# Moving a router's part boundaries, one batch's gather to GpSimd's queue and its transpose to TensorE

## The reference, cut to what matters

```python
x = L0_attn_x                                  # (8, 512, 128): 8 batches of 512 tokens
x = x + attn(layernorm(x))                     # 16 heads, causal softmax, then sa @ Wp + bp
h = layernorm(x)
shared = (silu(h @ shared_gate.T) * (h @ shared_up.T)) @ shared_down.T
probs = sigmoid(h @ router_w.T + routing_bias) # 8 experts, the top 2 of each token
w = the two probs over their sum, 0 for the other six experts
combined = sum over e of w[:, e] * ((silu(h @ gate_w[e]) * (h @ up_w[e])) @ down_w[e])
return x + shared + combined
```

## Time and profile before

| what | value |
|---|---|
| median of 3 runs | 767.33 us (763.23 to 767.85) |
| the profiled execution | 765.89 us |
| its span, first to last instruction | 764.1 us |
| PE, DVE, ACT, Pool busy | 659.3, 538.8, 459.9, 304.5 us |
| matmuls | 5426 |

### The profile page before, as it was taken

The page is one execution under the profiler, slowest core; times in us unless marked ns, Lnnn a source line. Parts: engine busy times, 40 slices in busy tenths (PEclk is TensorE's granted clock), DMA queues, the critical chain, the costliest instruction groups (busy, mean ns, idle before and its releaser), DMA issues. The chain is left out here.

```text
span 764.1 us, 16403 instructions
## 1 busy us (share of the span) xinstructions
PE 659.3 (86%) x5426; PEld 398.2 (52%) x5426; DVE 538.8 (71%) x1900; ACT 459.9 (60%) x817; POOL 304.5 (40%) x508
## 2 busy tenths in 40 slices
PE   7478999999989998999999998996788789888920
PEld 6354455545545554454555554553377677577610
DVE  6799777787788788878778778762057755667914
ACT  3366667757757766667867766673475546556600
POOL 3493512314223223463322322367600067666671
PEclk9799999999999999999999999999899899999955
DMA  9102335411110311230210210134155543764322
GB/s 249 46 2 64 90 108 149 144 57 57 46 56 29 74 36 36 75 114 26 80 51 29 59 32 28 40 78 103 36 120 113 113 108 111 142 120 123 101 67 83
DMA packets 104849, 61.07 MB, mean 80 GB/s; under 512 B 45960, under 2 KB 96544, under 8 KB 104768
## 3 DMA queue, kind: packets, MB, share of 16 engines
q1 hardware_dynamic: 68336, 29.34, 15.9%
q10 hardware_dynamic: 32336, 22.29, 9.5%
q0 software_dynamic: 4096, 8.40, 4.3%
HBM read 19.88 MB, written 31.06 MB: 67 GB/s over the span
## 5 line engine op out<-in xcount | busy, mean ns | idle before, releaser
L1256 ACT ACTIVATE p_sb<-bank,inv_scale 128x512 f32<-128x512 f32 (+1 forms) x384 | 221.9, 614 | 34.3 <-PE bank L1018 27.1
L1370 DVE CUSTOM_DVE_ANT_0 junk<-bank,causal 128x512 bf16<-128x512 f32 (+3 forms) x512 | 221.2, 483 | 23.6 <-PE bank L995 23.3
L904 POOL TENSOR_SCALAR_AFFINE_SELECT p_sb<-p_sb 128x384 f32<-128x384 f32 x128 | 66.9, 522 | 303.5 <-ACT p_sb L1256 303.3
L1017 PE MATMUL bank<-ql,ah 128*128 128x512 f16 (+3 forms) x512 | 153.7, 300 | 0.0
L1018 PE MATMUL bank<-qh,al 128*128 128x512 f16 (+3 forms) x512 | 153.2, 300 | 0.0
L995 PE MATMUL bank<-ah,qh 128*128 128x512 f16 (+3 forms) x512 | 132.1, 302 | 23.6 <-DVE low L1370 22.2
L1016 PE MATMUL bank<-qh,ah 128*128 128x512 f16 (+3 forms) x512 | 147.5, 301 | 1.2 <-ACT p_sb L1256 1.2
L1342 DVE TENSOR_TENSOR ql<-bank,qh 128x512 f16<-128x512 f32 x128 | 88.5, 691 | 68.9 <-ACT qh L1221 65.2
L1221 ACT ACTIVATE qh<-bank 128x512 f16<-128x512 f32 x128 | 76.4, 597 | 63.3 <-PE bank L960 61.7
L1546 DVE SCALAR_TENSOR_TENSOR al<-bank,gu_scale,ah 128x512 f32<-128x512 f32 x69 | 51.6, 748 | 72.9 <-ACT ah L1287 56.6
L995 PEld LDWEIGHTS bank<-ah,qh 128*128 128x128 f16 x512 | 50.0, 98 | 82.2 <-DVE low L1370 49.7
(11 more groups left out here) (234 smaller groups left out, 1162.0 us busy)
## 6 DMA issues: line engine op xcount, KB each, us to landing
o_dram<-oT ACTq DMA_DIRECT2D x32, 256.0 KB, 2.3
ys_dram<-ql ACTq DMA_DIRECT2D x25, 256.0 KB
xs_dram<-causal ACTq DMA_DIRECT2D x6, 832.0 KB, 4.6
wst<-in_Wkqv SPq DMA_DIRECT2D x8, 264.0 KB, 5.3
x_sb<-in_x SPq DMA_DIRECT2D x8, 256.0 KB, 6.0
o_all<-o_dram SPq DMA_DIRECT2D x8, 256.0 KB
r_all<-r_dram SPq DMA_DIRECT2D x8, 256.0 KB
x_dram<-rows SPq DMA_DIRECT2D x8, 256.0 KB, 2.3
```

Of the source, the lines that this page charges most:

```text
L904: nc.gpsimd.affine_select(out=three, in_=three, compare_op=ALU.is_ge, fill=0.0, base=0, pattern=[[0, 3], [1, P]], channel_multiplier=-1).t ...
L1017: nc.tensor.matmul(bank, m.ah[:, keys], ql[:, s, c * P:N], start=False, stop=False)
L1256: nc.scalar.activation(p_sb[v % P_RING][:, S_AT[k]:S_AT[k] + S_WIDTH[k]], m.psum[S_BANK[k]][:, 0:S_WIDTH[k]], ACT.Exp, scale=m.inv_scale[: ...
L1370: last = nc.vector.tensor_tensor_reduce(out=junk[:, (3 * u + k) % 2, at:at + w], in0=m.psum[M_BANK[(3 * u + k) % 2]][:, at:at + w], in1=m. ...
```

## The change

It does five things. The parts become 3, 2 and 3 batches. The steps behind a batch's attention are put into other slots, most of them earlier and several into one; the sort's pieces get slots of their own. For batch 7 the gather of sums and products and the spread of the inverses are issued by Pool's own queue, in slot 144, and SP no longer has them. Batch 7's normed rows are transposed by PE (`late`, slot 150) and copied from the bank by ACT and DVE (`late_copy`, slot 151) in place of the store and the two transposing loads. The logits of batch 6 stand in slot 141 and their exponentials are taken in slot 152, together with batch 7's; the buffer `lg` gets two halves for that.

The slots that come of it (batch b < 6: from slot 29 + 16 b):

| step | before | after |
|---|---|---|
| rinv, mult, proj, stats of batch b | +2, +4, +6, +6 | +0, +2, +4, +6 |
| aggr, newton, norm, split, logits of b | +8, +10, +11, +14, +18 | +6, +6 and +7, +8, +10, +14 |
| sort of the first part | 67, 71 | 79 (three pieces), 80, 81, 82, 83 |
| its sends | 76 to 83 (16) | 88 to 99 (24) |
| sort of the second part | 115, 119 | 111 (three pieces), 112, 113, 114, 115 |
| its sends | 124 to 135 (24) | 120 to 127 (16) |
| batch 6: mult, proj, norm, split, logits | 129, 131, 136, 139, 143 | 127, 129, 133, 135, 141 |
| batch 7: rinv, mult, proj | 142, 145, 147 | 144, 144, 148 |
| batch 7: norm, logits; third sort, place, first send | 148, 154; 155, 158, 159 | 149, 152; 153, 156, 157 |

```diff
@@ -32,7 +32,7 @@
 HN_RING = 6
 W_BOUND = 4096.0
 GU_BOUND = 32.0 / W_BOUND ** 2
-SPLITS = ((0, 8), (8, 20), (20, 32))
+SPLITS = ((0, 12), (12, 20), (20, 32))
 PARTS = len(SPLITS)
 CHUNK = P // E
 CHUNKS = tuple(tuple((t, min(t + CHUNK, t1)) for t in range(t0, t1, CHUNK)) for t0, t1 in SPLITS)
@@ -448,14 +448,18 @@
 
 SORTS = 7
 PLACE_LATE = -(-(PV_AT - LOW_AT) // GROUP)
-STEPS = {"rinv": 2, "mult": 4, "proj": 6, "stats": 6, "aggr": 8, "newton0": 10, "newton1": 10, "newton2": 10, "norm": 11, "split": 14, "logits": 18}
-LAST_STEPS = {"rinv": 1, "mult": 4, "proj": 6, "stats": 6, "aggr": 6, "newton0": 7, "newton1": 7, "newton2": 7, "norm": 7, "split": 8, "logits": 13}
-PART_STEPS = {"sort": 22, "weigh": 26, "count": 27, "rank": 30, "place": 30, "expert": 34, "send": 31}
-LAST_PART_STEPS = {"sort": 14, "count": 16, "weigh": 16, "rank": 17, "place": 17, "expert": 18, "send": 18}
+STEPS = {"rinv": 0, "mult": 2, "proj": 4, "stats": 6, "aggr": 6, "newton0": 6, "newton1": 7, "newton2": 7, "norm": 8, "split": 10, "logits": 14}
+LATE_LOGITS = 16
+LAST_STEPS = {"rinv": 3, "mult": 3, "proj": 7, "stats": 7, "aggr": 7, "newton0": 8, "newton1": 8, "newton2": 8, "norm": 8, "late": 9, "late_copy": 10, "logits": 11, "split": 12}
+PART_STEPS = {"sort": 18, "weigh": 22, "count": 23, "rank": 26, "place": 26, "expert": 30, "send": 27}
+LAST_PART_STEPS = {"sort": 12, "weigh": 13, "count": 14, "rank": 15, "place": 15, "expert": 16, "send": 16}
+SORT_LATE = ((0, 0, 0, 1, 2, 3, 4), (0, 0, 0, 0, 1, 1, 1))
 
 
 def step_at(name, b):
 
+    if (name, b) == ("logits", B - 2):
+        return step_at("rinv", b) - STEPS["rinv"] + LATE_LOGITS
     return PV_AT + H - GROUP + 2 + H * b + (STEPS if b < B - 1 else LAST_STEPS)[name]
 
 
@@ -467,12 +471,17 @@
 
 def sort_at(k, g):
 
-    return part_step_at("sort", g) + k // 4 * (GROUP if g < PARTS - 1 else 1)
+    return part_step_at("sort", g) + SORT_LATE[g == PARTS - 1][k]
 
 
 def batch_at(name, t):
 
     return next((b for b in range(B) if step_at(name, b) == t), None)
+
+
+def late_at(name, t):
+
+    return step_at(name, B - 1) == t
 
 
 def part_at(name, t):
@@ -805,9 +813,11 @@
                 inverses = m.r_dram[b * P:(b + 1) * P, :].rearrange("(h c) n -> h (c n)", h=H)
                 sp.dma_start(r_all[:, :], inverses.unsqueeze(1).to_broadcast([H, DH, N])).then_inc(r_placed, 16)
 
-            def turn_rows(b):
+            def store_rows(b):
                 sp.wait_ge(xl_ready, b + 1)
                 sp.dma_start(m.x_dram[b * N:(b + 1) * N, :].rearrange("(t p) d -> p t d", p=P), rows[:, b % HN_RING, :, :]).then_inc(x_stored, 16)
+
+            def turn_rows(b):
                 sp.wait_ge(x_stored, 16 * (b + 1))
                 if b >= 1:
                     sp.wait_ge(x_turned, 16 * 2 * b)
@@ -853,12 +864,8 @@
                     for b in range(t0 // TB, t1 // TB):
                         sp.wait_ge(rows_sent[b], 16 * 2 * TB)
                 if q == X_RING:
+                    store_rows(B - 2)
                     turn_rows(B - 2)
-                    gather_products(B - 1)
-                if q == X_RING + 1:
-                    spread_inverses(B - 1)
-                if q == LAST_TURN:
-                    turn_rows(B - 1)
                 if q >= X_RING:
                     sp.wait_ge(gate_up, quad_ends[q - X_RING])
                 for k, x in enumerate((xsh, xsl)):
@@ -905,9 +912,25 @@
                     one = p[:, P_AT[1]:P_AT[1] + P]
                     nc.gpsimd.affine_select(out=one, in_=one, compare_op=ALU.is_ge, fill=0.0, base=0, pattern=[[1, P]], channel_multiplier=-1).then_inc(p_masked, 1)
 
+                if late_at("rinv", t):
+                    for k in range(2):
+                        pool.wait_ge(o_stored[k], 16 * H // GROUP // 2 * B)
+                    pool.wait_ge(rinv_ready, B - 1)
+                    pool.wait_ge(on_ready, B - 1)
+                    heads = m.o_dram[(B - 1) * H // GROUP * P:B * H // GROUP * P, :].rearrange("(h c) n -> h c n", h=H)
+                    pool.dma_start(sums[:, :], heads[:, DH, :]).then_inc(late_sums_placed, 16)
+                    pool.dma_start(o_all[:, :], heads[:, 0:DH, :]).then_inc(late_o_placed, 16)
+                    pool.wait_ge(rinv_ready, B)
+                    pool.dma_start(m.r_dram[(B - 1) * P:B * P, :], rinv[:, :]).then_inc(late_r_stored, 16)
+                    pool.wait_ge(late_r_stored, 16)
+                    inverses = m.r_dram[(B - 1) * P:B * P, :].rearrange("(h c) n -> h (c n)", h=H)
+                    pool.dma_start(r_all[:, :], inverses.unsqueeze(1).to_broadcast([H, DH, N])).then_inc(late_r_placed, 16)
+                if late_at("mult", t):
+                    pool.wait_ge(late_r_placed, 16)
+                    pool.wait_ge(late_o_placed, 16)
                 if (b := batch_at("mult", t)) is not None:
-                    pool.wait_ge(r_placed, 16 * (b + 1))
-                    pool.wait_ge(o_placed, 16 * (b + 1))
+                    pool.wait_ge(r_placed, 16 * min(b + 1, B - 1))
+                    pool.wait_ge(o_placed, 16 * min(b + 1, B - 1))
                     if b >= 1:
                         pool.wait_ge(t_filled, T_TURN["proj", b - 1] + 1)
                     nc.gpsimd.tensor_tensor(onT[:, :], o_all[:, :], r_all[:, :], ALU.mult).then_inc(on_ready, 1)
@@ -1048,11 +1071,18 @@
                     for i in range(TB):
                         last = nc.tensor.matmul(bank_t[:, i * P:(i + 1) * P], onT[:, i * P:(i + 1) * P], m.wp[:, :], start=True, stop=True)
                     last.then_inc(t_filled, 1)
+                if late_at("late", t):
+                    turn("late", 0)
+                    pe.wait_ge(hn_ready, B)
+                    for i in range(TB):
+                        last = nc.tensor.transpose(bank_t[:, i * P:(i + 1) * P], hn[:, i, :], m.ident[:, :])
+                    last.then_inc(t_filled, 1)
                 if (b := batch_at("logits", t)) is not None:
                     turn("logits", b)
                     if b == 0:
                         pe.wait_ge(scale_chain, SCALE_LINKS)
-                    pe.wait_ge(x_turned, 16 * 2 * (b + 1))
+                    if b < B - 1:
+                        pe.wait_ge(x_turned, 16 * 2 * (b + 1))
                     for i in range(TB):
                         at = slice((b * TB + i) * P, (b * TB + i + 1) * P)
                         logits = bank_t[:, i * E:(i + 1) * E]
@@ -1111,8 +1141,10 @@
                 if u >= DEEP:
                     pe.wait_ge(gu_ready, u - DEEP + 1)
                 if unit.shared:
-                    if unit.half == 0:
+                    if unit.half == 0 and unit.batch < B - 1:
                         pe.wait_ge(x_turned, 16 * 2 * (unit.batch + 1))
+                    elif unit.half == 0:
+                        pe.wait_ge(t_taken, T_TURN["late", 0] + 1)
                     for kind, bank in ((0, GB), (1, UB)):
                         at = E * EW + kind * I + unit.half * P
                         last = three(m.psum[bank[u % DEEP]], 0, wh[:, at:at + P], wl[:, at:at + P], xh[:, seg(unit.batch, N)], xl[:, seg(unit.batch, N)])
@@ -1294,11 +1326,16 @@
                     quad, q = unit.quad, unit.quad.q
                     act.wait_ge(yst_ready, q + 1)
                     act.dma_start(m.ys_dram[quad.part][quad.rows, :].rearrange("(j p) d -> p j d", p=P), yst[:, q % X_RING, 0:quad.n * D].rearrange("p (j d) -> p j d", d=D)).then_inc(ys_stored[q % X_RING], 16)
+                if late_at("late_copy", t):
+                    act.wait_ge(t_filled, T_TURN["late", 0] + 1)
+                    act.wait_ge(wl_ready, KINDS * (E + 1))
+                    nc.scalar.activation(xh[:, seg(B - 1, N)], bank_t[:, :], ACT.Copy, scale=LIFT).then_inc(late_xh_ready, 1)
                 if t >= FFN_AT:
                     split_rows(t)
-                if (b := batch_at("logits", t)) is not None:
-                    act.wait_ge(t_taken, T_TURN["logits", b] + 1)
-                    nc.scalar.activation(ex[:, seg(b, TB), :], lg[:, :, :], ACT.Exp, scale=-1.0).then_inc(ex_ready, 1)
+                for b in range(B):
+                    if step_at("logits", max(b, B - 1) if b == B - 2 else b) == t:
+                        act.wait_ge(t_taken, T_TURN["logits", b] + 1)
+                        nc.scalar.activation(ex[:, seg(b, TB), :], lg[:, b % 2, :, :], ACT.Exp, scale=-1.0).then_inc(ex_ready, 1)
 
         @block.vector
         def _(dve):
@@ -1329,6 +1366,11 @@
                     dve.wait_ge(t_filled, T_TURN["rank", g] + 1)
                     n = len(CHUNKS[g]) * P + E
                     nc.vector.tensor_copy(ranks[:, 0:n], bank_t[:, 0:n]).then_inc(t_taken, 1)
+                if late_at("late_copy", t):
+                    dve.wait_ge(late_xh_ready, 1)
+                    dve.wait_ge(t_filled, T_TURN["late", 0] + 1)
+                    dve.wait_ge(wl_ready, KINDS * (E + 1))
```

(6 more changed lines are left out.)

18 lines of the change are left out of this document (9 added, 9 removed).

## The result

The changed kernel took 759.2 us, the median of 4 runs (758.33 to 760.1), beside 767.38 us for the kernel before (763.23 to 767.85, 4 runs): a ratio of 0.9898, 95% interval 0.9861 to 0.9935, so 8.2 us faster. The forecast was 750.0, range 739 to 759. The profiled execution took 758.33 us, its span is 756.5; before it was 765.9 and 764.1, so in the traces the gain is 7.6.

The account below looks back on a forecast made before the run. PE was taken as the bound, with Pool setting its pace for 40 us. Terms 2 + 14.6 + 3.9 - 3.3 = 17.2 us gained took 765.9 to 748.7, as a median 750.1; range 739 to 759.

Parts of the forecast that it names:

- (a): Attention, slots 29 to 127: moved DVE steps and sort pieces gain 2 us; bounds 5.3 gained, 3 lost.
- The groups with sorts: Sign for attention: groups of four slots that hold sort pieces would take 15 to 16 us.
- (b): Slots 128 to 139: no sends among the last masks, second unit at 537.8 instead of 552.42, 14.6 us gained; bounds 8, 17.
- the one wait near 1 us at proj: Sign for slots 128 to 139: of PE's three waits on Pool only one near 1 us stays, at proj.
- (c): Second unit to batch 7's proj: waits go, Pool issues the transfers, proj in slot 148; 3.9 us gained, bounds -2, 7.
- X + 12.4: When DVE has batch 7's inverses done: 12.4 us after X, the end of the last values.
- (d): Batch 7's proj to the third part's places: 35 us for 9 units, 3.3 lost; bounds 2 gained, 8 lost.
- R1: Rival: gain given back behind attention, or Pool still two slots behind at the last masks; 757 us, chance 0.19.
- The sign given for the clock: Between slots 149 and 157 the granted clock would fall below 1.0 in one or two windows.
- (e): The rest, held free: larger first part, earlier third-part sends and fetches change nothing at slot 178 or the tail; 0 us.
- the rule that was weighed against the change: Batch 7's proj chain: transfers issued from Pool stand while DVE runs two-port instructions, so it would wait for DVE's copies.
- R4: Rival: slower than before, Pool's two plain transfers cost 8.6 us each above 3.1, deciding from 17.2; 772 us, chance 0.04.

Follow-up runs that it names:

- experiment 5: Changed kernel with the step, sort and send slots of before for batches 0 to 5 and the first two parts: 728.92 us, ratio 0.9795 to the kernel before.
- experiment 2: Changed kernel with the parts of before, 2, 3 and 3 batches: 758.04 us, ratio 0.9892 to the kernel before.
- experiment 11: Changed kernel with batch 7's four transfers on SP's queue, run beside the changed kernel on one chip: 721.63 us, ratio 0.9691 against 0.9744.
- experiment 1: Changed kernel with batch 7's four transfers issued by SP's queue instead of Pool's: 753.76 us, ratio 0.983 to the kernel before.
- experiments 3 and 4: Changed kernel, third part's 24 fetches as plain SP transfers: 730.21 us; changed kernel, those fetches held until the last unit's downs are done: 761.81 us.
- 9, 10: Changed kernel and kernel before, both unaltered, on a chip of the second kind: 725.17 us against 744.39, ratio 0.9744.

## Why the forecast was off

- **(a) Attention.** 2 gained was forecast. On the result's chip slot 124's projection comes 1.0 us earlier, on the other chip 2.0 *later*; but 0.4 of the one and 1.4 of the other had arisen by slot 28, ahead of every moved step. From slot 28 to 124 it is 366.6 us before and 365.9 changed, with 1.4 us of extra time in one slot of before (4.55 instead of 3.15); on the other chip it is 363.8 and 364.3, and experiment 5 has 364.1. So the step is worth nothing that these traces can tell. On the other chip slots 68 to 75, from which the sort went, take 29.2 instead of 33.1 us, and slots 80 to 87, to which it came, 34.5 instead of 30.0; slots 32 to 35, with batch 0's proj and the bundled statistics, take 16.1 instead of 15.1. The groups with sorts were not at 15 to 16 us but at 15.6 to 17.8.
- **(b) The last masks.** 14.6 was forecast for (b) alone: 15.2 at the second unit less (a) is 14.2, on the other chip 12.4 and 2.0, thus 14.4. Right in size, place and mechanism, the one wait near 1 us at proj included; what experiment 2 adds is that the earlier sends do most of it (11 us), not the part's size (3.1).
- **(c) To batch 7's proj.** 3.9 was forecast. The stretch takes 23.65 us and a slot of 2.0 more is done, so 1.5 gained, 2.5 on the other chip. The inverses were ready at 549.46, where X + 12.4 had them; the mis-sized term is Pool's two transfers in line, taken at 2.1 + 1.0 us each, 6.2 in all, measured 8.7. SP does the same in 5.3 from issue to `onT`, and that is 3.5 us of the whole time on one chip (experiment 11) and about 5 by experiment 1.
- **(d) To the places.** -3.3 was forecast: 32.0 us for 9 slots instead of 35, against 37.7 for 12, is -0.4, and -2.1 on the other chip. R1's premise, that these hand-overs eat the gain, fell with it. The sign given for the clock came true: it was granted at 0.66 from 559 to 564 us and at 0.54 from 584 to 589.
- Up to here the sum is 16.3 us on the result's chip: 15.2 + 1.5 - 0.4, close to the forecast 17.2. That is luck in part: (c) fell 2.4 short, and (d) came out 2.9 better.
- **(e) Free.** This is the step that failed: "the earlier sends of the third ... change nothing at slot 178", and of the tail "the change leaves it as it is". It was put at 0 and was -8.7 on the result's chip (16.3 down to 7.6). In its place the runs show that PE isn't free there: it stands idle by issue, mostly beside Pool's indirect transfers, 28.2 us before and 36.7 changed. The difference, 8.5, is near the 8.7, but stage by stage the two don't match. From slot 159 to 178 the lead falls by 1.5 us with 4.1 more of this idle time. From 178 to 203 it falls by 3.3 with 0.8 less of it; there the granted clock counts as well. In slots 178 to 190 it is 0.94, where it was 1.00 before, and 316 matmuls keep PE busy for 28.9 us, where 307 took 26.4. It is at 0.50, the lower level of 1.2 GHz, from 648.3 to 652.4 us; from 642 to 648 PE had stood for 4.7 us in four gaps by issue. The stretches, first before, then two after (us, busy PE, PEld, DVE, ACT, POOL, clock, DMA share, GB/s):

```profile
661.31:691.23 29.92, 26.40 (x307) 22.82 (x305) 19.27 (x35) 16.00 (x29) 18.75 (x19) 1.00 0.60 126
...
648.70:680.07 31.37, 28.92 (x316) 25.53 (x314) 20.32 (x37) 16.15 (x29) 18.95 (x18) 0.94 0.56 107
648.30:652.40 4.10, 4.10 (x31) 3.50 (x30) 2.92 (x5) 2.09 (x4) 1.45 (x2) 0.50 0.16 39
```

From slot 203 on it falls by 1.6 with 5.2 more. And experiment 2, as fast as the changed kernel, has only 28.5 us of it from 600 us on. How much of the 8.7 is owed to this idle time is therefore not shown.

The tail was also misread. The forecast took the fetches and the last additions for all of it; but on chips of the second kind the end comes 9.1 to 9.5 us behind the last fetch of these kernels, and on the result's chip 15.2 before and 18.2 changed. There PE's last downs set the end: when the last fetch ends (738.3), three batches' shared additions are still to come (742.55 to 746.74), where before had two behind 748.9. The fetches start 10.2 us earlier, but only 1 us sooner against the units.

On the other chip the same term is +5.8: there is no such idle time, and the earlier sends free PE of its wait at slot 178, 4.2 of it. Both signs lay in rows of before that the forecast passed over: PE's rows with "issue" beside Pool's fetches, and the last send of the third part, at 648.74, with the unit that reads its rows 7.4 us behind it; on the other chip that distance is 7.5 and PE waits in it.

- **The range** ended at 759, the result is 759.2. R1 has nearly this time for another reason; no rival named PE's own supply.

What holds PE is settled as far as this: in the tail it takes Pool's fetches beside it (experiments 3 and 4: no idle time by issue without them), it is not the bytes, and some chips don't have it (9, 10). Whether it is the indirect form or Pool's queue stays open, since the runs meant to tell came on chips of the second kind.

How PE is held is open too. The sequencer waits for nothing that the profile shows, so a late supply of instructions is one reading. The profile's page has a queue of instructions with 47 packets and 0.77 MB, 16 KB each; the Trainium skill, Runtime: NRT & Kernel Launch, section "Instruction fetch mechanics", says that each engine's sequencer refills its buffer in blocks of that size over a DMA queue of its own, and that this is mostly hidden. The size agrees. But the trace speaks against a late block in the tail: these packets take 0.9 to 1.6 us each in both traces of the result's chip, and 0.9 to 2.1 on the other; and from 713.5 to 742 us, while PE takes up an instruction every 0.7 us, no queue of instructions moves anything:

```profile
q0 software_dynamic: 673, 1.38, 19.3%
q1 hardware_dynamic: 528, 0.26, 3.1%
```

These are all the queues of that stretch. Why attention has 0.3 us or less of this idle time beside 39 us of indirect sends is open, and so is why the changed kernel has more of it between slots 159 and 178. As for the rule that was weighed against the change (the Trainium skill, SBUF — State Buffer, section "SBUF: two separate sides", on transfers issued from GpSimd beside VectorE's two-port modes): Pool's transfers were dearer than SP's by 3.1 us for two, far from R4's 17.2, and no run tells whether any of that is DVE's doing.
